# Delta-rule layer: small products of one batch each in place of products over a zero-padded 128x128 block

## The reference, cut to what matters

```python
q = _l2norm(q); k = _l2norm(k); v = v * beta[..., None]; kb = k * beta[..., None]
A = jnp.where(tri_strict, -(kbc @ jnp.swapaxes(kc, -1, -2)), 0.0)
T = solve_triangular(eye - A, eye, lower=True)          # 32 x 32 for one chunk
u = T @ vc;  w = T @ kbc
def step(S, inp):                                        # over the 16 chunks, in order
    q_i, k_i, u_i, w_i = inp
    attn = jnp.where(causal, q_i @ jnp.swapaxes(k_i, -1, -2), 0.0)
    u_adj = u_i - w_i @ S
    o_i = q_i @ S + attn @ u_adj
    return (S + jnp.swapaxes(k_i, -1, -2) @ u_adj, o_i)
```

## Time and profile before

| what | value |
| --- | --- |
| median of three runs | 4633.0 us |
| profiled execution, its own time | 4642.6 us |
| its span | 4640.9 us |
| mean granted TensorE clock | 0.926 |
| PE busy | 3893.3 us, 84% of the span |
| DVE, ACT, POOL busy | 2555.7, 1942.6, 2042.9 us |
| DMA engines, mean rate | 99 GB/s |

### The profile page before, as it was taken

The page is one execution under the profiler, slowest core; times in us unless marked ns, Lnnn a source line. Parts: engine busy times, 40 slices in busy tenths (PEclk is TensorE's granted clock), DMA queues, the critical chain, the costliest instruction groups (busy, mean ns, idle before and its releaser), DMA issues. The chain is left out here.

```text
span 4640.9 us, 64911 instructions
## 1 busy us (share of the span) xinstructions
PE 3893.3 (84%) x23106; PEld 2714.6 (58%) x23106; DVE 2555.7 (55%) x4545; ACT 1942.6 (42%) x3555; POOL 2042.9 (44%) x2062
## 2 busy tenths in 40 slices
PE   4577897889999818976999889788888888999995
PEld 2364785457676508963455455466666666656663
DVE  4365754455555483236776622389988887412223
ACT  2315142423333202224666512388888887112222
POOL 3440555322222205652333211188999999332223
PEclk9688998999999958988999989899999999899997
DMA  4582743110000247964554311111111111822224
GB/s 120 174 259 76 235 106 86 57 56 10 19 10 14 66 153 208 296 182 141 163 151 126 89 64 37 47 37 46 51 51 50 50 48 51 268 96 42 46 46 129
DMA packets 334387, 459.36 MB, mean 99 GB/s; under 512 B 71430, under 2 KB 246086, under 8 KB 329942
## 3 DMA queue, kind: packets, MB, share of 16 engines
q1 hardware_dynamic: 311430, 424.32, 30.0%
q0 software_dynamic: 22512, 30.36, 3.5%
q10 hardware_dynamic: 128, 0.52, 0.0%
HBM read 314.58 MB, written 140.51 MB: 98 GB/s over the span
## 5 line engine op out<-in xcount | busy, mean ns | idle before, releaser
L3565 POOL TENSOR_TENSOR mamba_hC<-mamba_h_t,mamba_cb 128x512 f32<-128x512 f32 x512 | 672.8, 1346 | 78.4 <-DVE mamba_h_t L3078 72.2
L3078 DVE TENSOR_TENSOR_SCAN mamba_h_t<-mamba_dA,mamba_pB 128x512 f32<-128x512 f32 x512 | 596.2, 1206 | 116.1 <-PE mamba_pB L3456 51.5
L3456 PE MATMUL mamba_pB<-ident,mamba_dBT 128*128 128x128 f32 x2048 | 328.0, 284 | 61.3 <-DVE mamba_h_t L3078 55.1
L3254 ACT ACTIVATE mamba_dA<-mamba_delta,mamba_a_neg 128x512 f32<-128x512 f32 x512 | 358.0, 716 | 20.3 <-DVE mamba_h_t L3078 19.5
L3456 PEld LDWEIGHTS mamba_pB<-ident,mamba_dBT 128*128 128x128 f32 x2048 | 239.3, 144 | 198.3 <-issue 105.5
L3465 PE MATMUL mamba_pY<-ident,mamba_hC 128*128 128x128 f32 x2048 | 320.1, 280 | 17.9 <-POOL mamba_hC L3565 16.4
L1911 POOL TENSOR_SCALAR mqa_prob<-mqa_prob,mqa_rinv 128x128 f32<-128x128 f32 (+3 forms) x256 | 137.0, 535 | 424.6 <-DVE mqa_rinv L1687 423.6
L3245 ACT ACTIVATE mamba_dBT<-mamba_eT,mamba_b_t 128x512 f32<-128x512 f32 x384 | 274.9, 716 | 0.1
L2350 DVE TENSOR_REDUCE mha_nmax<-mha_pM 128x1 f32<-128x384 f32 (+3 forms) x352 | 216.1, 636 | 104.1 <-PE mha_pM L2658 101.1
L1501 POOL DMA_INDIRECT top_sum<-top_y,top_xg x71 | 110.4, 1555 | 351.7 <-ACT top_y L1290 341.4
L3465 PEld LDWEIGHTS mamba_pY<-ident,mamba_hC 128*128 128x128 f32 x2048 | 246.9, 145 | 27.3 <-POOL mamba_hC L3565 26.5
(11 more groups left out here) (621 smaller groups left out, 9143.9 us busy)
## 6 DMA issues: line engine op xcount, KB each, us to landing
expert_w<-in_L_ffn_W SPq DMA_DIRECT2D x48, 1024.0 KB
delta_shared<-delta_w SPq DMA_DIRECT2D x64, 576.0 KB, 5.0
mamba_cb<-mamba_c SPq DMA_DIRECT2D x128, 256.0 KB, 3.2
mha_qkT<-mha_parts_d SPq DMA_DIRECT2D x96, 256.0 KB, 5.0
delta_w<-delta_wst SPq DMA_DIRECT2D x32, 576.0 KB, 2.8
expert_w<-in_L_ffn_W SPq DMA_DIRECT2D x48, 256.0 KB
top_w<-in_L_ffn_w SPq DMA_DIRECT2D x24, 512.0 KB
top_slots<-top_y SPq DMA_DIRECT2D x1, 9159.0 KB, 37.4
```

What stands on the lines that cost most here:

```text
L3078: nc.vector.tensor_tensor_scan(h_t[:, n % RH, :], dA[:, n % RA, :], pB[n % 2][:, :], 0.0, ALU.mult, ALU.add).then_inc(z["scan_ready"], 1)
L3254: nc.scalar.activation(dA[:, n % RA, :], delta[:, a % 2, ct, :], ACT.Exp, scale=a_neg[:, ct, s:s + 1])\
L3456: last = nc.tensor.transpose(pB[n % 2][:, tok(t)], dBT[:, r % RS, t, ct * P:(ct + 1) * P], c.ident[:, :])
L3565: nc.gpsimd.tensor_tensor(hC[:, n % RO, :], h_t[:, n % RH, :], cb[:, r % RC, :], ALU.mult)\
```

## The change

- Scores, inverse product, output and Gram blocks are computed as one small product for each batch, on the 32 partitions (or 32 columns) of that batch alone. The zero padding is gone: `attn`, `attnT`, `mask`, `te` and `gs` hold 32 columns for each block instead of 128.
- `attn` and `attnT` are tiles of their own now. `te` is one tile, in the place of `table`, with room for all 16 chunks of both halves. It isn't cleared. Its loads come as part 0 (4 chunks) and part 1 (12 chunks), both after the store of the inverses; none is left in the recurrence.
- A group of the Gram section has four chunks instead of two: four groups a half, each with two ACT copies and four stores, and in the first half four table stores after each.
- The mask is loaded with four DMAs, one for each batch.
- The key scale is gone from ACT's copy of the scores, which becomes one instruction instead of four, and from DVE's copy to `kr`, which becomes a plain copy. In their place DVE's copy to `ua` multiplies by it.

The diff, with lines that stay the same left out:

```diff
@@ -4060,7 +4060,7 @@
-        mask = sc.sb("mask", [P, P])
+        mask = sc.sb("mask", [P, CH])
@@ -4092,6 +4092,8 @@
+        attn = sc.sb("attn", [P, 2, H, CH])
+        attnT = sc.sb("attnT", [P, 4, H, CH])
@@ -4110,21 +4112,22 @@
-        S_of, oT, sqo, yn0, res, otok, xtok, yn1, attnT, og, attn = (
+        S_of, oT, sqo, yn0, res, otok, xtok, yn1, og = (
...
-            take(2, D), take(4, H, P), take(4, 2, D), take(2, H, P))
+            take(2, D), take(4, 2, D))
...
-        systems = lambda flat: flat.rearrange("p (a s i) -> p a s i", a=2, s=4 * H)
-        te = (systems(table[:, :, :].rearrange("p g x -> p (g x)")[:, 0:8 * H * P]), systems(logits_of[:, :]))
+        te = table[:, :, :].rearrange("p g x -> p (g x)")[:, 0:HF * NCH * H * CH]\
+            .rearrange("p (f s i) -> p f s i", f=HF, i=CH)
...
-        gs = by_chunk[:, :, :].rearrange("p (a h) j -> p a h j", h=H)
+        gs = by_chunk[:, :, :].rearrange("p n i -> p (n i)")[:, 0:8 * H * CH]\
+            .rearrange("p (a t h i) -> p a t h i", a=2, t=4, h=H)
@@ -4143,14 +4146,14 @@
-                 "y_scale", "yn_ready", "y_out", "te_clear", "dch", "pch")
+                 "y_scale", "yn_ready", "y_out", "dch", "pch")
...
-        LOADS = 3 + 4 + H + 1 + 3 + 1 + H + P // DH + 1 + 2
+        LOADS = 3 + 4 + H + 1 + 3 + 1 + H + P // DH + HB + 2
@@ -4229,7 +4232,8 @@
-                load(mask[:, :], w["chunk_masks"][:, 6, :])
+                for b in range(HB):
+                    load(mask[lanes(b), :], w["chunk_masks"][lanes(b), 6, lanes(b)])
@@ -4329,13 +4333,11 @@
-                def load_inverses(hf, i):
-                    if i >= 2:
-                        sp.wait_ge(z["ua_ready"], HF * (4 * (i - 1) - 1) + hf + 1)
+                def load_inverses(hf, part):
+                    some = slice(4 * H, NCH * H) if part else slice(0, 4 * H)
...
-                        sp.dma_start(te[hf][lanes(bb), i % 2, :, lanes(bb)],
-                                     systems_by_row(t_d, hf, bb)[:, 4 * H * i:4 * H * (i + 1), :])\
-                            .then_inc(te_in[hf][i % 2], 16)
+                        sp.dma_start(te[lanes(bb), hf, some, :], systems_by_row(t_d, hf, bb)[:, some, :])\
+                            .then_inc(te_in[hf][part], 16)
@@ -4383,20 +4385,20 @@
-                    for i in range(NCH // 2):
-                        n = NCH // 2 * hf + i
+                    for i in range(NCH // 4):
+                        n = NCH // 4 * hf + i
...
-                            sp.dma_start(systems_by_row(g_d, hf, bb)[:, 2 * i * H:(2 * i + 2) * H, :],
-                                         gs[lanes(bb), 2 * (n % 2):2 * (n % 2) + 2, :, lanes(bb)]
-                                         .rearrange("p a h i -> p (a h) i")).then_inc(g_st[n % 2], 16)
+                            sp.dma_start(systems_by_row(g_d, hf, bb)[:, 4 * i * H:(4 * i + 4) * H, :],
+                                         gs[lanes(bb), n % 2, :, :, :].rearrange("p t h i -> p (t h) i"))\
+                                .then_inc(g_st[n % 2], 16)
...
-                            store_table(FG // 2 + 2 * i)
-                            store_table(FG // 2 + 2 * i + 1)
+                            for g in range(4):
+                                store_table(FG // 2 + 4 * i + g)
...
-                        sp.wait_ge(g_st[i], 64 * 4 * (hf + 1))
+                        sp.wait_ge(g_st[i], 64 * 2 * (hf + 1))
@@ -4428,7 +4430,6 @@
-                    sp.wait_ge(z["te_clear"], hf + 1)
@@ -4455,8 +4456,6 @@
-                    if ch % 4 == 3 and ch // 4 + 2 < NCH // 4:
-                        load_inverses(hf, ch // 4 + 2)
@@ -4549,10 +4548,8 @@
-                        nc.vector.tensor_tensor(kr[:, 2 * i:2 * i + 2, :].rearrange("p n (h d) -> p (n h) d", d=DH),
-                                                bank[6 + n % 2][:, :].rearrange("p (n d) -> p n d", d=DH),
-                                                rqk[:, 1, 2 * i:2 * i + 2, :].rearrange("p n h -> p (n h)").unsqueeze(2)
-                                                .to_broadcast([P, 2 * H, DH]), ALU.mult).then_inc(z["kr_ready"], 1)
+                        nc.vector.tensor_copy(kr[:, 2 * i:2 * i + 2, :].rearrange("p n d -> p (n d)"), bank[6 + n % 2][:, :])\
+                            .then_inc(z["kr_ready"], 1)
@@ -4623,7 +4620,10 @@
-                    nc.vector.tensor_copy(ua[:, s % 2, :], bank[5][:, 0:D]).then_inc(z["ua_ready"], 1)
+                    ch, hf = divmod(s, HF)
+                    nc.vector.tensor_tensor(by_head(ua[:, s % 2, :]), by_head(bank[5][:, 0:D]),
+                                            rqk_of[:, hf, 1, ch, :].unsqueeze(2).to_broadcast([P, H, DH]), ALU.mult)\
+                        .then_inc(z["ua_ready"], 1)
@@ -4753,15 +4753,15 @@
-                    for i in range(NCH // 2):
-                        n = NCH // 2 * hf + i
+                    for i in range(NCH // 4):
+                        n = NCH // 4 * hf + i
...
-                            of = gs[:, 2 * (n % 2):2 * (n % 2) + 2, :, :].rearrange("p t (g c) j -> p t g c j", c=2)
-                            nc.scalar.activation(of[:, :, :, odd, :],
-                                                 bank[2 + 2 * (n % 2) + odd][:, :].rearrange("p (t g j) -> p t g j", t=2, j=P),
+                            of = gs[:, n % 2, :, :, :].rearrange("p t (g c) j -> p (t g) c j", c=2)
+                            nc.scalar.activation(of[:, :, odd, :],
+                                                 bank[2 + 2 * (n % 2) + odd][:, 0:8 * CH].rearrange("p (x j) -> p x j", j=CH),
@@ -4798,14 +4798,11 @@
-                    ch, hf = divmod(s, HF)
...
-                    for h in range(H):
-                        last = nc.scalar.activation(attn[:, s % 2, h, :], bank[2][:, h * P:(h + 1) * P], ACT.Copy,
-                                                    scale=rqk_of[:, hf, 1, ch, h:h + 1])
-                    last.then_inc(z["attn_raw"], 1)
+                    nc.scalar.activation(attn[:, s % 2, :, :].rearrange("p h i -> p (h i)"), bank[2][:, 0:H * CH], ACT.Copy)\
+                        .then_inc(z["attn_raw"], 1)
@@ -4938,16 +4935,17 @@
-                    for i in range(NCH // 2):
-                        n = NCH // 2 * hf + i
+                    for i in range(NCH // 4):
+                        n = NCH // 4 * hf + i
...
-                        for t in range(2):
+                        for t in range(4):
...
-                                k = chunk(k_t, h // 2, 2 * i + t, half(h))
-                                at_col = (2 * t + h // 2) * P
-                                last = nc.tensor.matmul(bank[2 + 2 * (n % 2) + h % 2][:, at_col:at_col + P], k, k,
-                                                        start=True, stop=True)
+                                k = chunk(k_t, h // 2, 4 * i + t, half(h))
+                                at_col = (2 * t + h // 2) * CH
+                                for bb in range(HB):
+                                    last = nc.tensor.matmul(bank[2 + 2 * (n % 2) + h % 2][lanes(bb), at_col:at_col + CH],
+                                                            k[:, lanes(bb)], k[:, lanes(bb)], start=True, stop=True)
@@ -4962,7 +4960,7 @@
-                    pe.wait_ge(z["g_ready"], NCH * (hf + 1))
+                    pe.wait_ge(z["g_ready"], NCH // 2 * (hf + 1))
@@ -5015,8 +5013,9 @@
-                        last = nc.tensor.matmul(bank[2][:, h * P:(h + 1) * P], k_of(s, half(h))[h // 2], q_of(s, half(h))[h // 2],
-                                                start=True, stop=True)
+                        for bb in range(HB):
+                            last = nc.tensor.matmul(bank[2][lanes(bb), h * CH:(h + 1) * CH], k_of(s, half(h))[h // 2][:, lanes(bb)],
+                                                    q_of(s, half(h))[h // 2][:, lanes(bb)], start=True, stop=True)
@@ -5038,24 +5037,26 @@
-                    i = ch // 4
-                    if ch % 4 == 0:
-                        pe.wait_ge(te_in[hf][i % 2], 64 * (i // 2 + 1))
+                    if ch in (0, 4):
+                        pe.wait_ge(te_in[hf][ch // 4], 64)
...
-                        last = nc.tensor.matmul(bank[5][:, cols(h)], te[hf][:, i % 2, H * (ch % 4) + h, :],
-                                                res[:, s % 2, cols(h)], start=True, stop=True)
+                        for bb in range(HB):
+                            last = nc.tensor.matmul(bank[5][lanes(bb), cols(h)], te[lanes(bb), hf, H * ch + h, :],
+                                                    res[lanes(bb), s % 2, cols(h)], start=True, stop=True)
...
-                        last = nc.tensor.matmul(bank[3 + hf][:, cols(h)], attnT[:, s % 4, h, :], ua[:, s % 2, cols(h)],
-                                                start=False, stop=True, skip_group_check=True)
+                        for bb in range(HB):
```

(10 more changed lines are left out.)

## The result

The kernel after takes 4607.05 us (median of five runs, 4603.4 to 4617.4) against 4635.9 us for the kernel before (five runs too, the three shown ahead among them): a ratio of 0.9945 with a 95% interval of 0.9929 to 0.9961. That is 0.55% faster, 25 us by the ratio and 29 us by the two medians. The forecast was 4621 with a range of 4604 to 4645. The time lies in the range and the sign is right, but the gain is more than twice the 12.3 us that I had worked out.

The account below looks back on a forecast made before the run. TensorE, working in program order and hardly idle, was taken to bound the recurrence. Terms +1.5 + 0 - 4 + 2.8 - 12.6 = -12.3 us brought the median from 4633.0 to 4621 us, range 4604 to 4645.

Parts of the forecast that it names:

- Start, +1.5: Kernel start: four mask loads instead of one delay the first matmul, which waits for the last load, by 1.5 us.
- Gram, first half, 0: First half's Gram section: pace set by POOL's 16 tables and their stores; no change, bounds -3 and +2 us.
- Gram, second half, -4: Second half's Gram section: fewer rounds of stores bring the reload and DVE's start sooner, -4 us, bounds 0 and -8.
- the wait for the larger last store: Second half's Gram section: the reload waits for a last store that is now larger, +1.6 us.
- Inverse loads, +2.8: Recurrence entry: extra inverse loads delay the chunk-3 operands PE needs at step 4, +2.8 us once, bounds 0 to +5.
- Recurrence, 28 x 0.45: Recurrence steps on PE: small records at 25 ns save 0.45 us a step over 28 steps, -12.6 us.
- my lower bound of 14: Recurrence's small records: four tiles of 64 columns side by side give 14 ns a record, saving about 1.3 us a step.
- the 0.12 us that I added for changes of form: Recurrence: odd scores, and output ahead of the projection, cost 0.12 us beyond their record issue.
- Rival 1: Recurrence: small records cost 32 ns, a step loses 0.1 us, whole 4636 us (4645 at 36 ns); chance 17%.
- Rival 2: Recurrence: no floor per record, four tiles truly side by side, 28 x 1.3 us saved, whole 4597 us; chance 12%.
- Rival 3: Recurrence: row groups writing one PSUM bank take turns, 58 ns a record, about +45 us, whole 4680 us; chance 8%.
- Rival 4: Recurrence: the granted clock falls on small products, once every two steps, +22 us, whole 4643 us; chance 10%.

Follow-up runs that it names:

- e3: Kernel after with the inverse loads of chunks 8 to 15 back at steps 6 and 7 instead of the entry: 4609.6 us, ratio 0.9953.
- e4: Kernel after with each of the 16 small inverse products of a step issued twice: 4642.6 us, ratio 1.0018 against before.
- e9: Kernel of e7 with the chunk-3 operand load also moved ahead of the token rows in SyncE's queue: 4595.2 us, ratio 0.9916 against before.
- e5: Kernel after with the inverse products reordered, the four heads of one batch behind each other: 4622.2 us, ratio 0.9969 against before.
- e6: Kernel after with the odd heads' scores issued ahead of the inverse product: 4603.6 us, ratio 0.9929 against before.
- e7: Kernel after with late inverse loads (chunks 8 to 15) and odd scores ahead of the inverse: 4602.6 us, ratio 0.9921 against before.
- e10: Kernel after with the second half's 2 MB store of filtered values at the entry cut to a sixteenth: 4606.8 us, ratio 0.9939 against before.
- e1: Kernel before with only the recurrence's scores, inverse and output as small products, in the old padded tiles: 4617.6 us, ratio 0.9959.
- e8: Kernel before with only the key scale moved to the copy to ua, one unscaled ACT copy: 4640.2 us, ratio 1.0010.
- e11: Kernel before with only the Gram section's products made small, in old groups, copies and stores: 4640.3 us, ratio 1.0011.

## Why the forecast was right, and its size wrong

The marks of the two profiles add up: until the Gram section of the first half -0.6 us, that section to its reload -1.5, from there to the second half's Gram +4.5, that section -6.0, its reload to the store of the inverses -3.0, entry -3.7, recurrence -18.7, together -29.1 us. Not all of these are the change:

- **The +4.5** arises while PE computes the first half's filters and waits for their tables from memory. The kernels built on before have -2.2 to +1.1 there. Those built on after have 0.0 to 0.8 (e3, e4, e9), 3.5 to 3.8 (e5, e6, e7) and 6.8 (e10). Whether the change costs something here is open.
- **The -3.0** is inside the scatter: this stretch takes 93.3 to 97.6 us in the kernels built on before and 91.5 to 95.8 in those built on after.
- **Of the -3.7**, 1.6 are the clock.

By the terms of the forecast:

- **Start, +1.5.** The first matmul comes at 20.37 for 19.01, 1.4 later; when the Gram section starts, at 158.87 for 159.51, nothing is left of it that can be told. That start scatters from 156.9 to 163.0 over all kernels.
- **Gram, first half, 0:** -1.5, in the bounds, but unchanged code takes 56.4 to 57.4 us there in before, e1 and e8, so most of it may be scatter.
- **Gram, second half, -4:** -6.0, and -5.5 alone. The mechanism, fewer rounds of stores, fits the rows, and the smaller copies of ACT go with it. The term that was off is the wait for the larger last store. I had added 1.6 us for it; from the last store's issue to the reload it takes 1.75 us where it took 1.24, so 0.5 more. e11 shows that the products are not the gain. PE does stand without a releaser here as well, 2.9, 5.7 and 2.5 us with 128 products between, and ACT's second copy waits 1.7 us for it.
- **Entry, not in my sum:** -3.7. Ahead of the first step PE computes four blocks of scores with ACT's copies between them, and I priced the products only inside the steps. 2.1 us of it are theirs, by the kernels of like clock.
- **Inverse loads, +2.8:** 3.0 by e3, with the reservation made there. The statement that the gains of steps 0 to 3 are lost was right, and more than that: from step 0 to step 6 the kernel after takes 39.5 us against 32.5.
- **Recurrence, 28 x 0.45.** The path was right, the size was not: this is the term that failed. The term was 25 ns for a small record, 17.8 and 16 were measured, near my lower bound of 14 and not midway between the rows of larger tiles. Also, the 0.12 us that I added for changes of form did not appear (16 odd scores in 0.26 us). At 1.19 us a step 28 steps give 33 us; I had bounded it at 1.3. What the profile shows of it without the loads is 18.7 + 3.0 = 21.7. The other 11 us are the stall without a releaser, which I had not thought of, the time at 1.2 GHz behind both stalls, and some 4 us in the steps behind step 6. Of these, 2.4 are one step at a low clock, and the rest are steps 0.1 to 0.6 us longer than the shortest. That the time still fell into the range is in part luck: with 33 us for the steps and the other terms as they stood, my sum would have given 4600, under the range's 4604. The stall and the clock brought it back.
- **Rival 1** (32 ns) fell by e4 and the step's rows. **Rival 2** was the nearer one in price, by my own sign too (0.57 us from inverse to odd scores, where 0.8 was the forecast and 0.5 the rival), but its 4597 left out what faster products run into. **Rival 3** (row tiles take turns) is refuted in the form of its premise: products of four row groups that write one bank cost 17.8 ns, and 40 if the same tile of the array is used again (e5), against the 58 that I had worked out for taking turns. The rule of the Trainium skill, "TensorEngine Tiling (Array Packing)", "Gotcha 1: PSUM Pressure", by which different row tiles cannot access one bank at a time, is not what this trace shows, where each wrote its own partitions. The 25 ns of the Trainium skill, "TensorE: Matmul & The Clock Gate", "Wait — 56ns, not 53.3ns?", is undercut as well, by 17.8 and 16 ns start to start in the recurrence and by 12 in the Gram section (128 products in 1.56 us). I had chosen between the ends by rows that lay beside that figure.
- **Rival 4** (the clock falls on small products): the granted clock is 1.00 from 640 to 735 us in the kernel after, with the small products in every step. It fell behind idle stretches of PE, and once without one, at 0.54 from 617 to 620 us, which cost 2.4 us. Before has two such falls without small products, of 1.5 us each, so the cause that I named is not shown. Over 600 to 740 us the mean is 0.99, and I had asked for under 0.9.

## What to carry to other kernels

Where a block-diagonal product is padded with zeros, one product for each block on its own rows and columns is worth its larger number if neighbours in program order use different tiles of the array; order the loops so. When the compute gets cheaper, look at once for the load that the first steps reach too early: here one position in a queue was worth 5 us of the recurrence (e9 against e7), and the end of an earlier stall 1 us. And count instructions where DMA is full: four times the records can stall on their own program. Before you credit a short stretch to a change, look whether unchanged products in it ran at the same clock: 1.6 of 3.7 us at the entry were that.

## What the runs showed of the hardware

- A pair of f32 records of a 32x32 by 64 product costs 35.6 ns when the neighbours use other tiles of the array, and 81 in the same tile (after and e5, clock 1.00).
- 64x32 by 32 products cost 16 ns a record on one row half at a clock of 1.00 and 23 at 0.50; where the two halves and two banks alternate, 12 at 0.50 (weight loads 11).
- At the entry, with the DMA engines full, PE stood for 2.8 to 4.3 us without a releaser in every kernel with small products in the recurrence, and for 1.05 us at most when the 2 MB store was cut to a sixteenth (e10).
- The DMA queue q8 brings TensorE's program, one packet for some 256 records (24 packets for 6112 records, 32 for 8160), and the stalls stand 127 to 128 products apart or a multiple of it.
- After the two stalls of the kernel after the granted clock was 0.5, and one step took 6.4 us, most of it at that clock, in place of 4.2.
